# Cross attention of a two-layer decoder: column maxima spread over eleven key tiles, value products in pairs, a ring of seven or eight exponentials

## What is computed

```python
q = (x @ W_q).reshape(b, n, HEADS, DIM_HEAD)          # 8 heads in layer 0, 16 in layer 1, 64 wide
k = (context @ W_k).reshape(b, j, HEADS, DIM_HEAD)
v = (context @ W_v).reshape(b, j, HEADS, DIM_HEAD)
sim = jnp.einsum('bihd,bjhd->bhij', q, k) * scale
sim = jnp.where(mask[:, None, None, :], sim, max_neg)  # layer 0 only
attn = jax.nn.softmax(sim, axis=-1)
out = jnp.einsum('bhij,bjhd->bihd', attn, v).reshape(b, n, INNER)
return out @ W_o + b_o
```

## Time and profile before

| | |
|---|---|
| median of 3 runs | 3352.18 us (3350.86 to 3354.28) |
| the profiled execution | 3353.5 us, of which its span (first to last instruction) 3351.8 us |
| mean granted TensorE clock over the span | 0.932 |
| PE busy | 2940.3 us, 88% of the span |
| DVE, POOL, ACT busy | 1892.8, 1663.3, 1304.6 us |
| main loop of cross attention, layer 0 (16 groups) | 579.3 to 1395 us |
| main loop of cross attention, layer 1 (32 groups) | 1686 to 3218 us |

### The profile page before, as it was taken

The page is one execution under the profiler, slowest core; times in us unless marked ns, Lnnn a source line. Parts: engine busy times, 40 slices in busy tenths (PEclk is TensorE's granted clock), DMA queues, the critical chain, the costliest instruction groups (busy, mean ns, idle before and its releaser), DMA issues. The chain is left out here.

```text
span 3351.8 us, 38244 instructions
## 1 busy us (share of the span) xinstructions
PE 2940.3 (88%) x12634; PEld 1724.7 (51%) x12634; DVE 1892.8 (56%) x3738; ACT 1304.6 (39%) x2299; POOL 1663.3 (50%) x1408
## 2 busy tenths in 40 slices
PE   6578886999899998687589999999999999999979
PEld 5323334555455555354455555555555555555457
DVE  2456665665756656433545565556555655565546
ACT  1144562444454443311144444444444444444410
POOL 0344202566565665610256666666666666666620
PEclk8688997999999999786699999999999999999979
DMA  8666503232322312000222232222312232222110
GB/s 276 140 163 153 126 2 92 62 95 49 99 53 61 93 47 50 32 0 0 81 66 49 65 99 68 50 65 64 101 47 65 70 75 73 65 64 66 30 51 26
DMA packets 113532, 245.81 MB, mean 73 GB/s; under 512 B 15366, under 2 KB 61703, under 8 KB 112184
## 3 DMA queue, kind: packets, MB, share of 16 engines
q1 hardware_dynamic: 107128, 219.82, 26.2%
q0 software_dynamic: 5696, 23.42, 2.6%
q10 hardware_dynamic: 512, 0.13, 0.0%
HBM read 107.31 MB, written 31.76 MB: 41 GB/s over the span
## 5 line engine op out<-in xcount | busy, mean ns | idle before, releaser
L987 POOL TENSOR_TENSOR ACC<-ACC,PR 128x512 f32<-128x512 f32 (+1 forms) x1056 | 1333.3, 1286 | 647.8 <-ACT PR L1161 645.8
L1161 ACT ACTIVATE PR<-banks 128x512 f32<-128x512 f32 (+1 forms) x832 | 478.6, 596 | 732.8 <-PE banks L1075 726.4
L1092 PE MATMUL banks<-PR,V 128*64 128x512 f32 (+1 forms) x2496 | 672.8, 622 | 0.9 <-ACT OT L1147 0.7
L1220 DVE TENSOR_REDUCE mx<-banks 128x2 f32<-128x800 f32 (+1 forms) x512 | 506.0, 988 | 230.2 <-PE banks L1046 227.3
L1046 PE MATMUL banks<-KH,QZ 128*128 128x400 f32 (+1 forms) x1536 | 500.1, 381 | 129.1 <-DVE mx L1220 63.4
L1074 PE MATMUL banks<-QA,KA 128*128 128x512 f32 (+1 forms) x1248 | 560.1, 449 | 4.6 <-DMA QB<-ROW 4.6
L1190 DVE TENSOR_TENSOR KB<-banks,KH 64x400 fp32r<-64x400 f32 (+1 forms) x384 | 219.7, 572 | 517.7 <-ACT KH L1120 514.0
L1075 PE MATMUL banks<-QB,KB 65*128 65x512 f32 (+1 forms) x1248 | 497.7, 399 | 0.0
L1046 PEld LDWEIGHTS banks<-KH,QZ 128*128 128x128 f32 x1536 | 273.1, 192 | 368.5 <-issue 141.6
L1074 PEld LDWEIGHTS banks<-QA,KA 128*128 128x128 f32 (+1 forms) x1248 | 232.2, 186 | 404.7 <-issue 260.3
L1161 ACT ACTIVATE PR<-banks,keybias 128x512 f32<-128x512 f32 (+1 forms) x416 | 272.9, 686 | 373.5 <-PE banks L1075 352.4
(11 more groups left out here) (228 smaller groups left out, 3000.4 us busy)
## 6 DMA issues: line engine op xcount, KB each, us to landing
KA<-KH SPq DMA_DIRECT2D x192, 400.5 KB, 6.7
CX<-ctx_split SPq DMA_DIRECT2D x8, 2403.0 KB, 10.7
WK<-wk_split SPq DMA_DIRECT2D x48, 256.0 KB, 5.7
WV<-wv_split SPq DMA_DIRECT2D x24, 512.0 KB, 3.7
QA<-QZ SPq DMA_DIRECT2D x96, 128.0 KB, 2.3
QB<-QZ SPq DMA_DIRECT2D x96, 128.0 KB, 2.4
first<-in_w_in SPq DMA_DIRECT2D x8, 1024.0 KB, 6.3
second<-in_w_out1T SPq DMA_DIRECT2D x8, 1024.0 KB, 8.9
```

The costliest lines, as they stand in the source:

```text
L987: pool.tensor_tensor(acc, other, PR[0:r, n % RING, :], ALU.add).then_inc(summed, 1)
L1092: last = pe.matmul(OB[h * DH:(h + 1) * DH, :], V[0:r, g % 4, s, h * DH:(h + 1) * DH], PR[0:r, (n + h) % RING, :], start=(s == 0), stop=(s ...
L1161: act.activation(PR[0:r, n % RING, :], SB[n % 3][0:r, :], ACT.Exp, bias=keybias[0:r, g // pairs, t:t + 1] if masked else 0.0).then_inc(pro ...
L1220: dve.tensor_reduce(mx[:, :, t, c], both[:, :, 0:w], AX.X, ALU.max).then_inc(mx_done, 1)
```

## The change

Five edits, all in `cross`:
1. The value products of key tiles t-2 and t-1 are issued one after the other at even t; tile 12's at t = 13.
2. RING is 7 in layer 0 and 8 in layer 1 (it was 6). To make room, keybias lies in `self.small` instead of a tensor of its own.
3. The maxima's blocks are spread over t = 1 to 11. The table `where` gives each its tile and its position in the tile (0 after the scores of head 0, 1 after those of head 1, 2 after the jobs, 3 after the value products). Layer 1: one pair at t = 1, two pairs at odd t (positions 0 and 2), one at even t (position 2). Layer 0: one product at t = 1, four at t = 4, else three.
4. DVE's side work is ordered anew: "sum" at t = 1 instead of 2; reciprocals at t = 2 to 5 and ahead of the maxima of positions 2 and 3 instead of behind them; the multiplication of OT and RD at t = 6, ahead of those maxima; the addition to X behind them; the mask steps at t = 0, 11, 12 and 13.
5. "row" at t = 12 instead of 11.

```diff
-        RING = 6
+        RING = 7 if masked else 8
...
-            if g >= 1 and t == 2:
+            if g >= 1 and t == 1:
                 jobs.append(("sum", g - 1, 0))
...
-            if g + 1 < G and t == 11:
+            if g + 1 < G and t == 12:
                 jobs.append(("row", g + 1, 0))
...
+        if masked:
+            where = [(1, 2)] + [(t, at) for t in range(2, 12) for at in ((0, 1, 2), (1, 2, 3), (0, 1, 2, 3))[2 if t == 4 else t % 2 == 0]]
+            blocks = [((i, h),) for i in range(NT * NC) for h in range(2)]
+        else:
+            where = [(1, 2)] + [(t, at) for t in range(2, 12) for at in ((0, 2), (2,))[t % 2 == 0]]
+            blocks = [((i, 0), (i, 1)) for i in range(NT * NC)]
...
-                            if t >= 1:
-                                s, r = t - 1, rows_of(t - 1)
-                                n = TP * g + 2 * s
+                            for s in range(t - 2, t) if t >= 2 and t % 2 == 0 else range(KT - 1, KT) if t == KT else ():
+                                r, n = rows_of(s), TP * g + 2 * s
                                 pe.wait_ge(probs, n + 2)
...
-                            for x in singles(g, t)[0:2]:
+                            for x in maxima_at(g, t, 0, 1):
                                 maximum(*x)
                             for x in at(g, t):
-                                job(x)
-                            for x in singles(g, t)[2:4]:
+                                if x[0] != "out":
+                                    job(x)
+                            if g >= 1 and 2 <= t < 2 + NT:
+                                invert(g - 1, t - 2)
+                            if g >= 1 and t == 2 + NT:
+                                normalise(g - 1)
+                            for x in maxima_at(g, t, 2, 3):
                                 maximum(*x)
-                                if x[1:] == (NT * NC - 1, 1):
-                                    maxima_end(x[0])
-                            if g >= 1 and 3 <= t < 3 + NT:
-                                invert(g - 1, t - 3)
-                            if masked and g % pairs == 1 and g // pairs + 1 < B and t in (4, 6, 8, 11):
-                                mask_step(g // pairs + 1, (4, 6, 8, 11).index(t))
+                            if t == max(where)[0] and g + 1 < G:
+                                maxima_end(g + 1)
+                            for x in at(g, t):
+                                if x[0] == "out":
+                                    job(x)
+                            if masked and g % pairs == 1 and g // pairs + 1 < B and t in (0, 11, 12, 13):
+                                mask_step(g // pairs + 1, (0, 11, 12, 13).index(t))
```

More of the change, by code:

```diff
@@ L823, in cross, with maxima_at @@
         place = {x: i for i, x in enumerate(order)}
-        def singles(g, t):
-            return [(g + 1, i, h) for i in range(2 * (t - 2), 2 * (t - 1)) for h in range(2)] if g + 1 < G and 2 <= t <= 9 else []
+        if masked:
[4 more added lines that the diff above has]
+            blocks = [((i, 0), (i, 1)) for i in range(NT * NC)]
+        def maxima_at(g, t, *at):
+            return [(g + 1, *x) for w, b in zip(where, blocks) for x in b if w[0] == t and w[1] in at] if g + 1 < G else []
         def sums_done(n):
@@ L856, in cross @@
             if masked:
-                keybias = sb("keybias", [P, B, KT])
+                keybias = self.small[:, 0:B * KT].rearrange("p (b t) -> p b t", b=B)
                 allowed = sb("allowed", [P, 2, B])
@@ L1076, in _ @@
                                           start=False, stop=True).then_inc(sc_ready, 1)
-                                for x in singles(g, t)[h:h + 1] if masked else singles(g, t)[0:2 - 2 * h]:
+                                for x in maxima_at(g, t, h):
                                     maximum(*x)
@@ L1080, in _ @@
                                 job(x)
-                            for x in singles(g, t)[2:3] if masked else singles(g, t)[2:4]:
+                            for x in maxima_at(g, t, 2):
                                 maximum(*x)
-                            if t >= 1:
-                                s, r = t - 1, rows_of(t - 1)
-                                n = TP * g + 2 * s
+                            for s in range(t - 2, t) if t >= 2 and t % 2 == 0 else range(KT - 1, KT) if t == KT else ():
+                                r, n = rows_of(s), TP * g + 2 * s
                                 pe.wait_ge(probs, n + 2)
@@ L1094, in _ @@
                                 last.then_inc(used, 1)
-                            for x in singles(g, t)[3:4] if masked else ():
+                            for x in maxima_at(g, t, 3):
                                 maximum(*x)
@@ L1227, in invert, with normalise @@
                         dve.reciprocal(part, part).then_inc(inverted, 1)
[L1228 to L1231, removed]
+                    def normalise(g):
+                        dve.wait_ge(inverted, NT * (g + 1))
+                        dve.wait_ge(o_done, g + 1)
+                        dve.tensor_tensor(OT[:, :], OT[:, :], RD[:, :], ALU.mult).then_inc(normed, 1)
                     def maxima_end(g):
@@ L1271, in _ @@
                         for t in range(KT + 1):
[L1272 removed]
+                            for x in maxima_at(g, t, 0, 1):
                                 maximum(*x)
                             for x in at(g, t):
[L1275 to L1283 removed]
+                                if x[0] != "out":
[5 more added lines that the diff above has]
+                            for x in maxima_at(g, t, 2, 3):
+                                maximum(*x)
+                            if t == max(where)[0] and g + 1 < G:
[5 more added lines that the diff above has]
+                                mask_step(g // pairs + 1, (0, 11, 12, 13).index(t))
                     for i in range(NT):
                         invert(G - 1, i)
+                    normalise(G - 1)
                     for x in after:
```

## The result

The changed kernel takes 3424.08 us in the median of 4 runs (3410.9 to 3429.82), the kernel before 3353.23 beside it (4 runs, 3350.86 to 3366.45): a ratio of 1.0192, 95% interval 1.0168 to 1.0216. It is 1.9% slower where 1.4% faster was forecast; the sign was wrong, and the time lies outside the range.

A forecast was written before the change was run, and what follows sets the result against it. The prediction took PE's own stream (busy 91 and 96% of the two main loops) as the bound. From 3353.5 us, - 94 + 68 - 22 gave 3305.5, less 1.3: forecast 3304 us, 1.4% faster, range 3265 to 3340.

The forecast's parts named there:

- Term 1: Value products in pairs: 0.34 us saved per joined tile, 2.05 us a group over 46 groups, 94 us less.
- Term 2: DVE's new order in layer 1: PE waits longer for reductions, +2.7 us an even and +2.1 an odd group, 68 us more.
- "sum" at t = 1: POOL's last addition of the group before ends some 4 us ahead: Among the edits priced at nothing: "sum" moved to t = 1 would not wait for POOL's addition, so 0 us.
- Term 3: The new order in layer 0: waits of 3.7 us in an ordinary group, 2.25 at t = 4; altogether 22 us less.
- The ring: Slots for exponentials, priced at nothing: pairs would stall with six slots; with seven and eight nothing waits.
- The slow one: Rival: each of four reciprocals ahead of a reduction costs layer 1 in full, 3.8 us a group; 3397 us, chance 0.09.
- The multiplication: Rival: OT x RD ahead of t = 6's reductions is held, up to 1.66 us, and PE feels it; 3350 us, chance 0.04.
- The pair saves nothing: Rival: other tiles' value products don't behave like tiles 11 and 12, so pairing gains nothing; 3400 us, chance 0.04.

The follow-up runs named there:

- e1: The kernel before with edits 1 and 2 alone (paired value products, ring of 7 and 8); 3442.93 us, ratio 1.0271.
- e5: The changed kernel with "sum" at t = 2, and reciprocals (t = 3 to 6) and multiplication (t = 7) behind the maxima; 3334.46 us, ratio 0.993.
- e7: e5 with value products of one tile at a time; 3323.0 us, ratio 0.9901.
- e8: e5 with "out" at t = 9 and 11, and the values of three-piece groups at t = 4, 5 and 7; 3273.79 us, ratio 0.9754.
- e9: e8 with the second maxima of t = 3 ahead of the copy of k(3) in DVE's order; 3237.08 us, ratio 0.965.
- e4: The kernel before with only "sum" moved to t = 1; 3441.61 us, ratio 1.026.
- e11: e9 with "sum" moved back to t = 1; 3279.56 us, ratio 0.9765.
- e2: The changed kernel with "sum" at t = 2, reciprocals at t = 3 to 6, multiplication at t = 7, still ahead of the maxima; 3347.23 us, ratio 0.9987.
- e3: The changed kernel with reciprocals and multiplication behind the maxima of positions 2 and 3; 3329.8 us, ratio 0.9933.
- e6: e5 with a ring of six slots (RING = 6); 3332.61 us, ratio 0.9929.

## Why the prediction was wrong, by its own steps

**Term 1 held as a length, not as a gain.** Blocks of 8 records take 1.87 us and those of 12 take 2.73, as forecast. The trace gives 0.34 us a block by the earlier trace rows and the same lengths after. (The estimate of 0.33 from the Trainium skill's "TensorEngine Tiling (Array Packing)", Key Properties, and "TensorE: Matmul & The Clock Gate", Single matmul latency, agrees with it in the sum; it has 0.166 each way, where the rows show 0.09 and 0.10, and the other 0.15 is that two tiles in a row take less than twice one.) But they end the cover that eleven single blocks gave. e1 has the pairs and is 2.7% slower; their worth depends on the rest of the order: 0 in e5 against e7, 7 us in e8, 51 in e9, always against single tiles that wait for ROW.

**Term 2 held, wait by wait.** In groups 24 and 25, start to start (forecast in brackets): t = 3 1.07 (0.95), t = 4 1.56 and 1.59 (1.5), t = 10 0.32 (0.35), t = 11 and odd groups' t = 7 0.79 (0.8), "row" 0.61 (0.55). Not foreseen were 0.20 at t = 9 and that the first product behind a wait takes 0.11 us more, four or five times a group.

**The step that failed is '"sum" at t = 1: POOL's last addition of the group before ends some 4 us ahead'.** It looked at what "sum" reads, not at where it writes. The rule was in the text on the kernel: a job waits for the last but one to be read. At t = 2 the last but one was k(1); at t = 1 it is q, whose two DVE copies (0.74 + 0.76) stand behind ACT's. It measures 1.24 us in each of 44 groups, 17 us of layer 0 and 37 of layer 1, and it was priced at nothing. e4 and e11 show it in two other surroundings, e2 takes it away. Against a forecast gain of 48 us, this 55 alone takes the gain away and leaves a tie. It is less than half of the miss of 120 us; the sign came with the rest, below.

**Term 3's waits held, its clock did not.** Layer 0's t = 4 was forecast at 2.25 us; PE's rows of group 3 of the changed kernel:

```profile
751.92 0.39 PE L1083 MATMUL banks<-QB,KB 65*128 65x512 f32 x1
754.56 0.42 PE L1054 MATMUL banks<-KH,QZ 128*128 128x400 f32 x1 [2.25 <-DVE mx L1224]
...
756.51 3.32 PE L1099 MATMUL banks<-PR,V 128*64 128x512 f32 x8
```

```profile
753.50:755.90 2.40, 1.34 (x11) 1.37 (x12) 2.30 (x8) 0.00 (x0) 1.54 (x2) 1.00 1.01 203
755.90:759.30 3.40, 3.40 (x12) 1.04 (x10) 1.21 (x3) 0.60 (x1) 0.00 (x0) 0.50 0.97 222
759.30:762.00 2.70, 2.70 (x17) 2.07 (x14) 1.74 (x5) 1.21 (x2) 0.44 (x1) 1.00 0.86 215
```

PE idles 2.25 us, the granted clock goes from 1.00 to 0.50 (from 2.4 to 1.2 GHz) for 3.4 us, and the pair of value products takes 3.32 us instead of 1.94. Group 3 is 2.4 us longer than before, group 4, where the same wait brought no fall, 0.7: a fall costs 1.7 us. Groups 8 and 12, of group 4's kind and as long as it before, have a fall and take 51.25 us each, 1.64 more than it. The changed kernel has 41 us at 0.5 in layer 0, in eleven stretches, each some 20 us into a group, where t = 4 lies: some 18 us of time, as an estimate from these groups. The kernel before has 41 too, in fewer groups, so only a part of it is net. With the wait at 1.3 us (e3) 10 us are left. Of the 43 us that layer 0 is worse than forecast, 17 are the sum's bank. Most of the rest is the falls, and a part is that term 3 took too large waits for the kernel before: 2.7 us in group 4 and 7.0 in group 2, by layer 1's work, where PE's idle rows add up to 1.84 and 5.24 (some 2.1 and 5.9 from start to start). A wait that isn't there can't be saved; over ten such groups that makes some 8 us. No run parts these.

**Layer 1's miss of 75 us:** 37 is the sum's bank; four more falls of the clock make some 6; what is left, 1.0 us a group, is the 0.11 behind each wait, 0.20 at t = 9 and up to 0.12 more on the others. This is a sum of steps in groups 24 and 25, not a run.

**The ring: "With six slots the pairs would stall" is wrong.** e6 runs six slots at the same time as e5.

**The rivals.** The slow one named the reciprocals: e3 shows that the place in front costs 94 us of 3424, or 87 by the ratios (reciprocals and multiplication together, with the falls of the clock that it brings), so the mechanism is there, but most of it stood in terms 2 and 3 already. The multiplication was not held: it takes 0.68 us in the median, 1.66 at the longest, and PE waits for it nowhere in groups 24 and 25. "The pair saves nothing" was refused by its length, and that was the wrong test: a length saved is not a time saved. I gave 0.11 to slower; the base of the error is that all the rivals were ways in which a priced edit could be mispriced, and none asked what an edit priced at nothing could cost.

## What to carry to other kernels

- When a step moves, ask for its output buffer as well as its inputs: who used the bank last but one, in the new order, and when does the reader let go of it.
- Work that is spread thinly on the bounding engine hides the latency of a helper. Before joining such blocks for their fixed cost (0.34 us here), list which wait each of them covers; join only together with an order that gives those waits another cover. Here the pairs cost 91 us alone. In the last version they gave 51 against single tiles, about as much as the wait for ROW that single tiles had there.
- On a helper engine with in-order work, put what the bounding engine waits for first, and then look at who waits for the work that was pushed back: e5 pushed the multiplication back until "out" waited for it, e8 gave "out" room.

## What was not expected of the hardware

- The granted clock fell behind waits of PE of 2.2 us in a loop that is otherwise full, and stayed at 0.5 for 3.4 us (6.8 in a few places). In e1, with 2.2 us at t = 4 of most groups, it is at 0.5 for 75 us of layer 1; in e9, with no wait over 0.7 us inside groups 24 and 25, for none of layer 1. It doesn't fall each time: groups 4 and 5 of layer 0 have the same 2.4 us wait and stay at 1.00. Nor does each fall stand behind such a wait: two of the changed kernel's five in layer 1 come at a group's end, where the last waits before them are of some 0.6 us.
- The first product of a pair of maxima behind a wait for DVE takes 0.29 us to the second in the changed kernel's layer 1, where one that didn't wait takes 0.18 (0.26 and 0.18 in the kernel before, medians).
